# Masked attention over tokens: where the normalised tokens of the next batch are turned, and a new order of the side work

## The chip, the cores and the metric

One core of a Trainium2 chip runs the whole program. The metric is the device time of one execution in microseconds (us); lower is better. The kernel before took 1127.6 us, the median of three runs (1122.86 to 1130.42).

## The reference

Eight batches of 1024 tokens with 256 features pass through one masked attention layer with eight heads of 32, all in float32:

```
h = max(layernorm(x), 0)
q, k, v = h @ Wq + bq, h @ Wk + bk, h @ Wv + bv
scores = q k^T / sqrt(32) + (1 - adj) * -1e9
out = x + softmax(scores) v @ Wo + bo
```

`adj` is one mask of 1024 by 1024 for all batches and heads.

## The kernel before

A batch has two phases, g = 0 and g = 1, of four heads each. A phase has 32 rows: eight query tiles of 128 tokens times four heads. Eight rows are a unit (two query tiles), so a phase has four units. I write a row as its number in the phase, 0 to 31.

For each row TensorE computes 128 x 1024 scores (`scores`, L726), VectorE adds the mask and takes the row's minimum (`mask_row`, L565), ScalarE takes the exponential (L476), TensorE turns the result in eight squares of 128 (`turn`, L759) into two PSUM tiles, and these are copied to SBUF: `turned_a` always by ScalarE (L481), `turned_b` by ScalarE in the rows that `ACT_COPIES` names (L486) and by VectorE in the others (L572). At the first row of the next unit TensorE multiplies the eight turned rows with the values (`heads`, L810). In front of each row's work stand the scores of a row some four places later (`SCORES_AHEAD`), so scores of row 35, which is row 3 of the next phase, are issued in row 31.

The sums of the exponentials are inverted and turned by VectorE at the unit's row `INV_ROW` (L601, L603), go by GpSimd's DMA queue to DRAM (L438) and come back spread over partitions (`inv_t`, four DMAs, L444); VectorE multiplies with them at row `NORM_ROW` of the next unit (`norm_heads`, L609). I call this the inverse chain.

Beside this, each phase holds the projections for the phase that follows, as steps of four pieces that `STEPS` puts at rows: `("qk", s, rows)` computes q (even s) or k (odd s) of the tokens' half s // 2, `("v", s, rows)` the values of a half, `("o", u, rows)` the output of unit u. All go through one PSUM bank, `ps_side`. For a qk step ScalarE writes the high part (L491), VectorE the low part (L577, `lo_done`), and SyncE (SP) then copies the parts to `q_stack` or `k_stack` by 16 DMAs, four for each head h (`stack_step`, L296). The scores of a phase's first four rows wait for their head's part of both halves; the k part of the second half is step qk 3, the last to come. For an o step VectorE adds the residual (`finish`, L615), and SP stores the result, waits until it is stored, and loads the next residual (`store`, L315 to L323).

SP works through its queue in the order of `STEPS`. The next batch's tokens `xn` come by one DMA of 1 MB after the stack of step qk 1 of phase 1 (`load_x`, L305). VectorE takes their moments (L591, L593) in phase 0 at the rows in `STATS`; GpSimd normalises them after unit 2 of phase 0 (`norm`, L412); TensorE turns them in 16 squares of 128 (`turn_ht`, L782) at rows 29 and 30 of phase 0 and 4 and 6 of phase 1 (`HT_ROWS`); ScalarE copies them with a maximum with 0 into `ht` (L508), four copies a batch. The steps qk and v of phase 1 read `ht` for the next batch.

## Time and profile before

| | us |
|---|---|
| median of three runs | 1127.6 |
| lowest, highest | 1122.86, 1130.42 |
| the profiled execution | 1129.57 |
| its span | 1127.8 |
| rows start (end of the start stage) | 33.5 |

The profiled execution's span is the time from its first to its last instruction. The granted TensorE clock was 0.992 of full over it. A batch in the middle of the program takes about 135.5 us, a phase some 67 to 68. In the timeline each line is start, time taken, engine, line, operation, tiles and count; PEld is TensorE's weight load, and since each matmul follows its load, the first weight load of a `turn` marks the start of a row on TensorE.

### The profile page before, as it was taken

How to read it: one execution, taken by the hardware profiler on the slowest of the kernel's cores; microseconds unless marked ns; L12 is line 12 of the kernel's file. 1: busy time of each engine (PE TensorE's matmuls, PEld its weight loads, DVE VectorE, ACT ScalarE, POOL GpSimd, SP SyncE). 2: the span in 40 equal slices, each digit the busy share in tenths (PEclk: the TensorE clock that was granted, in tenths of full speed). 3: DMA queues.
4: the chain of work that ended last, by engine and by line, in shares of the span. 5: the costliest groups of instructions: out<-in, count | busy, mean ns of one | idle time of the engine just before them, and what ended most of it. 6: DMA issues, size and time to landing. Idle time of an engine off the chain costs nothing.

```text
span 1127.8 us, 28288 instructions
## 1 busy us (share of the span) xinstructions
PE 1103.4 (98%) x10672; PEld 890.5 (79%) x10672; DVE 958.4 (85%) x1796; ACT 998.9 (89%) x1835; POOL 314.4 (28%) x508
## 2 busy tenths in 40 slices
PE   7989999999999999999999999999999999999997
PEld 5777887888778878887887887888877888878775
DVE  4788988988989888998889987898988988988884
ACT  2789999999989988999999998999989999999985
POOL 6364212232214212242212412124122142112222
PEclk9999999999999999999999999999999999999999
DMA  6842352425424253332524325243352424424101
GB/s 201 247 110 49 94 139 63 106 62 139 103 71 106 65 134 87 90 97 70 137 67 117 81 76 131 68 111 78 86 140 69 107 67 100 106 61 111 49 27 49
DMA packets 88037, 109.07 MB, mean 97 GB/s; under 512 B 24416, under 2 KB 50144, under 8 KB 87904
## 3 DMA queue, kind: packets, MB, share of 16 engines
q1 hardware_dynamic: 76704, 95.89, 31.6%
q0 software_dynamic: 11008, 11.13, 5.1%
q8 instruction: 86, 1.41, 0.6%
q14 instruction: 47, 0.39, 0.1%
q10 hardware_dynamic: 192, 0.26, 0.1%
HBM read 30.54 MB, written 9.44 MB: 35 GB/s over the span
## 4 chain that ended last, share of the span: by engine, by line
PE 37%; issue 29%; DMA 19%; POOL 10%; DVE 1%; ACT 1%; SPq 0%; POOLq 0%; DVEq 0%; ACTq 0%
PE ps_turn L759 11%; DMA inv_t<-inv_rows 9%; DMA inv_rows<-inv_turned 9%; PE ps_scores L726 9%; PE ps_heads L810 8%; POOL inv_t L444 6%; PE ps_side L766 3%; PE ps_side L793 2%; POOL xn L412 2%; PE ps_side L775 2%; POOL mask L451 2%; POOL ln_t L397 1%; DVE rows L565 1%; DMA mask<-in_adj 1%; ACT rows L476 1%
## 5 line engine op out<-in xcount | busy, mean ns | idle before, releaser
L565 DVE CUSTOM_DVE_ANT_0 rows<-ps_scores,mask 128x1024 f32<-128x1024 f32 x512 | 615.6, 1217 | 36.1 <-PE ps_scores L726 30.5
L476 ACT ACTIVATE rows<-rows,row_min 128x1024 f32<-128x1024 f32 x512 | 589.7, 1159 | 10.9 <-DVE row_min L565 10.8
L759 PE MATMUL ps_turn<-ident_r,rows_raw 128*128 128x128 f32 x4096 | 468.3, 258 | 13.3 <-DVE turned_b L572 7.9
L759 PEld LDWEIGHTS ps_turn<-ident_r,rows_raw 128*128 128x128 f32 x4096 | 402.0, 141 | 89.9 <-ACT rows L476 26.1
L481 ACT ACTIVATE turned_a<-ps_turn 128x512 f32<-128x512 f32 x512 | 307.6, 601 | 90.9 <-PE ps_turn L759 90.7
L726 PE MATMUL ps_scores<-k_stack,q_stack 128*128 128x512 f32 x1016 | 330.6, 424 | 0.5 <-DVE row_min L565 0.2
L572 DVE COPY turned_b<-ps_turn 128x512 f32<-128x512 f32 x312 | 214.9, 689 | 87.1 <-PE ps_turn L759 82.0
L438 POOL DMA_DIRECT2D inv_rows<-inv_turned x64 | 46.4, 725 | 635.5 <-DVE inv_turned L603 630.1
L444 POOL DMA_DIRECT2D inv_t<-inv_rows x256 | 135.5, 536 | 144.0 <-DMA inv_rows<-inv_turned 139.7
L726 PEld LDWEIGHTS ps_scores<-k_stack,q_stack 128*128 128x128 f32 x1016 | 159.3, 188 | 18.2 <-DVE row_min L565 8.8
L810 PE MATMUL ps_heads<-turned_a,v 128*32 128x256 f32 x2048 | 123.8, 382 | 0.4 <-ACT turned_a L481 0.4
L810 PE MATMUL ps_heads<-turned_b,v 128*32 128x256 f32 x2048 | 122.2, 379 | 0.0
L486 ACT ACTIVATE turned_b<-ps_turn 128x512 f32<-128x512 f32 x200 | 120.0, 600 | 0.4 <-PE ps_turn L759 0.4
L476 ACT ACTIVATION_READ_ACCUMULATOR rows<-rows,row_min 128x1 f32 x512 | 105.8, 207 | 0.0
L810 PEld LDWEIGHTS ps_heads<-turned_b,v 128*32 128x32 f32 x2048 | 66.6, 110 | 43.9
L810 PEld LDWEIGHTS ps_heads<-turned_a,v 128*32 128x32 f32 x2048 | 60.0, 109 | 38.0 <-ACT turned_a L481 0.5
L793 PE MATMUL ps_side<-wo,heads_t 128*128 128x256 f32 x256 | 72.6, 389 | 0.7 <-DVE heads_t L609 0.7
L775 PEld LDWEIGHTS ps_side<-wv,ht 128*128 128x128 f32 x496 | 67.6, 191 | 7.1 <-issue 0.4
L775 PE MATMUL ps_side<-wv,ht 128*128 128x128 f32 x496 | 69.4, 276 | 0.0
L766 PE MATMUL ps_side<-ht,wk 128*128 128x256 f32 x240 | 65.2, 395 | 0.0
L766 PE MATMUL ps_side<-ht,wq 128*128 128x256 f32 x240 | 64.9, 389 | 0.0
L793 PEld LDWEIGHTS ps_side<-wo,heads_t 128*128 128x128 f32 x256 | 47.6, 192 | 9.5 <-issue 1.2
(84 smaller groups left out, 592.0 us busy)
## 6 DMA issues: line engine op xcount, KB each, us to landing
q_stack<-q_hi SPq DMA_DIRECT2D x248, 64.0 KB, 2.0
q_stack<-q_lo SPq DMA_DIRECT2D x248, 64.0 KB, 2.1
k_stack<-k_hi SPq DMA_DIRECT2D x242, 64.0 KB, 2.0
k_stack<-k_lo SPq DMA_DIRECT2D x242, 64.0 KB, 2.0
res<-in_x SPq DMA_DIRECT2D x32, 256.0 KB, 2.8
inv_t<-inv_rows POOLq DMA_DIRECT2D x256, 32.0 KB, 2.3
out<-res SPq DMA_DIRECT2D x32, 256.0 KB, 2.4
xn<-in_x SPq DMA_DIRECT2D x7, 1024.0 KB, 6.9
```

What stands on the lines that cost most here:

```text
L444: pool.dma_start(inv_t[h * HEAD_DIM:(h + 1) * HEAD_DIM, :, :], by_head[h].partition_broadcast(HEAD_DIM)).then_inc(inv_in, 16)
L476: nc.scalar.activation(rows[:, k, :], rows[:, k, :], ACT.Exp, bias=row_min[:, k:k + 1], scale=-1.0, accum_out=row_sum[:, u % 2, j:j + 1]). ...
L481: nc.scalar.activation(turned[0][:, place(i // UNIT_ROWS, i % UNIT_ROWS)], ps_turn[0][:], ACT.Copy).then_inc(copied_a, 1)
L486: nc.scalar.activation(turned[1][:, place(i // UNIT_ROWS, i % UNIT_ROWS)], ps_turn[1][:], ACT.Copy).then_inc(copied_b, 1)
L565: nc.vector.tensor_tensor_reduce(out=rows[:, k, :], in0=ps_scores[n % 2][:], in1=mask[:, qt, :], scale=1.0, scalar=START_MIN, op0=ALU.add, ...
L572: nc.vector.tensor_copy(turned[1][:, place(i // UNIT_ROWS, i % UNIT_ROWS)], ps_turn[1][:]).then_inc(copied_b, 1)
L726: mm = nc.tensor.matmul(ps_scores[n % 2][:, c * BANK:(c + 1) * BANK], q_stack[g][:, h, qt * P:(qt + 1) * P], k_stack[g][:, h, c * BANK:(c ...
L759: tr = nc.tensor.transpose(ps_turn[half][:, k, :].bitcast(F32R), rows_raw[:, n % RING, kt * P:(kt + 1) * P], ident_r[:])
L766: mm = nc.tensor.matmul(bank[:, cols], w[n][:, k, g * P:(g + 1) * P], ht[:, k, s // 2 * BANK:(s // 2 + 1) * BANK][:, cols], start=(k == 0) ...
L775: mm = nc.tensor.matmul(bank[:, t * P:(t + 1) * P], ht[:, k, tok], w["v"][:, k, g * P:(g + 1) * P], start=(k == 0), stop=(k == DCH - 1))
L793: mm = nc.tensor.matmul(ps_side[:, t * DIM:(t + 1) * DIM], lhs, w["o"][:, g, :], start=(g == 0), stop=(g == PHASES - 1))
L810: mm = nc.tensor.matmul(ps_heads[h * HEAD_DIM:(h + 1) * HEAD_DIM, 0:UNIT_Q] .rearrange("p (t n) -> p t n", n=P), v[g][:, half * PARTS + kt ...
```

## The change

Batch 0's tokens are still turned by TensorE. For batches 1 to 7:

- `xn` is loaded in four DMAs of 256 KB with eight neighbouring tokens in each partition (`x_p`), one behind each head's part of the stack of step qk 2 of phase 1.
- Moments are taken at rows 0, 0, 1, 7, 7, 8, 8, 9. GpSimd normalises in two halves after units 0 and 1: it subtracts the mean with a maximum with 0, and multiplies in a second instruction, 16 a batch instead of 8.
- VectorE turns squares of 32 in four instructions of 128 x 512 (`turn_squares`), at the ends of rows 23, 24, 24 and 25 of phase 0. A ring of three buffers holds them; the fourth waits until the first is out.
- SP writes them to DRAM (`tokens_t`), two DMAs of 128 KB for each of the four, one pair behind each head's part of the stack of step qk 3 of phase 0, and reads the first half of `ht` back behind the last one, after all writes have landed. The second half is read at the start of phase 1. TensorE waits for these reads in place of `ht_done`.
- The 16 turns on TensorE and four copies on ScalarE a batch are gone.

For all batches: `inv_t` comes by two DMAs of 128 partitions, not four of 32; `INV_ROW` is 7 and `NORM_ROW` 3 (its place within the row moves from the end to the start); four late mask tiles go from GpSimd to VectorE at rows 9, 11, 13 and 15 of the first phase; `turned_b` is copied by ScalarE in 30 rows a batch instead of 25; the steps of phase 0 and the places in a row are laid newly.

```diff
-MASK_AHEAD = (4, 4, 3, 3, 3, 3, 3, 3)
-EXP_AHEAD = (1, 3, 2, 2, 2, 2, 2, 1)
+MASK_AHEAD = (4, 4, 4, 3, 3, 4, 4, 4)
+EXP_AHEAD = (1, 2, 2, 2, 2, 2, 2, 1)
...
-    (("qk", 0, (2, 2, 3, 3)), ("qk", 1, (5, 5, 6, 6)), ("o", 2, (9, 10, 11, 11)), ("qk", 2, (13, 13, 14, 14)),
-     ("v", 0, (17, 18, 19, 19)), ("qk", 3, (21, 21, 22, 22)), ("v", 1, (25, 26, 27, 27)), ("o", 3, (28, 29, 29, 30))),
+    (("v", 0, (1, 2, 3, 3)), ("qk", 0, (5, 5, 6, 6)), ("qk", 1, (9, 10, 11, 11)), ("qk", 2, (13, 13, 14, 14)),
+     ("o", 2, (17, 18, 19, 19)), ("qk", 3, (21, 21, 22, 22)), ("o", 3, (25, 26, 27, 27)), ("v", 1, (29, 29, 30, 30))),
...
-HT_ROWS = {(0, 29): 0, (0, 30): 1, (1, 4): 2, (1, 6): 3}
-HT_UNITS = {(0, 3): 2, (1, 0): 4}
...
+SQUARE_ROWS = (23, 24, 24, 25)
+PAIR, SQUARE_RING = 2, 3
...
 ACT_COPIES = (
-    (2, 5, 6, 10, 13, 14, 17, 18, 21, 22, 26, 28, 29),
-    (0, 1, 2, 10, 13, 14, 18, 21, 22, 26, 29, 30),
+    (2, 3, 5, 7, 8, 10, 11, 13, 15, 19, 21, 23, 26, 27, 29, 31),
+    (3, 5, 7, 8, 11, 13, 15, 16, 19, 21, 23, 27, 29, 31),
 )
...
+            def squares_out(b, pair):
+                n = (b - 1) * SQUARES + pair
...
+                sp.wait_ge(squares_done, n + 1)
+                for j in range(PAIR):
+                    block = pair * PAIR + j
+                    sp.dma_start(tokens_t[block * SQUARE:(block + 1) * SQUARE, :].rearrange("i (c n) -> c i n", c=PARTS),
+                                 squares[:, n % SQUARE_RING, j, :]).then_inc(ht_out[n % SQUARE_RING], 16)
+
+            def ht_back(b, c):
...
+                for k in range(DCH):
+                    sp.dma_start(ht[:, k, cols], tokens_t[k * P:(k + 1) * P, cols]).then_inc(ht_in[c], 16)
...
                     sp.wait_ge(scores_done, row(b, g, 0) + 1)
+                    if g == 1 and b + 1 < BATCH:
+                        ht_back(b + 1, 1)
                     for kind, s, _ in steps(g, b == 0, b == BATCH - 1):
                         if kind == "qk":
-                            stack(nb, ng, s)
...
+                            sp.wait_ge(lo_done, qk_step(nb, ng, s) + 1)
+                            for h in range(PARTS):
+                                stack_step(sp, ng, s, stacked["qk"[s % 2]][ng], range(h, h + 1))
+                                if g == 1 and s == 2 and b + 2 < BATCH:
+
+                                    sp.wait_ge(squares_done, (b + 1) * SQUARES)
+                                    load_x(b + 2, h)
+                                if g == 0 and s == QK_STEPS - 1 and b + 1 < BATCH:
+                                    squares_out(b + 1, h)
+                            if g == 0 and s == QK_STEPS - 1 and b + 1 < BATCH:
+                                ht_back(b + 1, 0)
...
+            def turn_squares(b, pair):
+                n, at = (b - 1) * SQUARES + pair, pair * PAIR * SQUARE
+                dve.wait_ge(normed, (b + 1) * TILES)
+                if n >= SQUARE_RING:
+
+                    dve.wait_ge(ht_out[n % SQUARE_RING], n // SQUARE_RING * PAIR * 16)
+                nc.vector.transpose(squares[:, n % SQUARE_RING].rearrange("p c (j t) -> p t c j", t=TILES),
+                                    xn[:, :, at:at + PAIR * SQUARE].rearrange("p t (c i) -> p t c i", i=SQUARE)
+                                    ).then_inc(squares_done, 1)
```

How the order moves, at three places. First SP's queue in phase 0 of a middle batch, at the store of unit 2 of the batch before. Before, the store stands between the stacks of k (step qk 1) and q (step qk 2):

```order
L296 DMA k_stack<-k_hi 32x512 x2
L296 DMA k_stack<-k_lo 32x512 x2
L317 DMA out<-res 128x2x256
L308 DMA res<-in_x 128x2x256
L296 DMA q_stack<-q_hi 32x512
L296 DMA q_stack<-q_lo 32x512
```

Now it stands between the stacks of q (step qk 2) and k (step qk 3), and the writes of the squares stand in the k stack:

```order
L311 DMA q_stack<-q_hi 32x512
L311 DMA q_stack<-q_lo 32x512
L329 DMA out<-res 128x2x256
L324 DMA res<-in_x 128x2x256
L311 DMA k_stack<-k_hi 32x512 x2
L311 DMA k_stack<-k_lo 32x512 x2
L346 DMA tokens_t<-squares 4x32x256 x2
L311 DMA k_stack<-k_hi 32x512 x2
L311 DMA k_stack<-k_lo 32x512 x2
L346 DMA tokens_t<-squares 4x32x256 x2
```

The store has moved one stack later, and three pairs of square writes stand ahead of the last head's k parts.

Then TensorE's queue at rows 29 to 31 of phase 0 of a middle batch. Before:

```order
L759 MATMUL ps_turn<-ident_r,rows_raw 128x128 x8
L782 MATMUL ps_heads<-ident_r,xn_raw 128x128 x4
L793 MATMUL ps_side<-wo,heads_t 128x256 x2
L759 MATMUL ps_turn<-ident_r,rows_raw 128x128 x8
L726 MATMUL ps_scores<-k_stack,q_stack 128x512 x2
L782 MATMUL ps_heads<-ident_r,xn_raw 128x128 x4
L793 MATMUL ps_side<-wo,heads_t 128x256
L759 MATMUL ps_turn<-ident_r,rows_raw 128x128 x8
L726 MATMUL ps_scores<-k_stack,q_stack 128x512 x4
```

Now:

```order
L821 MATMUL ps_turn<-ident_r,rows_raw 128x128 x8
L837 MATMUL ps_side<-wv,ht 128x128 x4
L821 MATMUL ps_turn<-ident_r,rows_raw 128x128 x8
L788 MATMUL ps_scores<-k_stack,q_stack 128x512 x2
L837 MATMUL ps_side<-wv,ht 128x128 x4
L821 MATMUL ps_turn<-ident_r,rows_raw 128x128 x8
L788 MATMUL ps_scores<-k_stack,q_stack 128x512 x4
```

Both groups of four token turns are gone, and step v 1 stands where step o 3 stood.

Last VectorE's queue from the low part of step qk 3, in row 23, to row 26 (ISA is `mask_row`). Now:

```order
L619 SCALAR_TENSOR_TENSOR k_lo<-ps_side,bk_col,k_hi 128x512
L646 STREAM_TRANSPOSE squares<-xn 128x8x64
L614 COPY turned_b<-ps_turn1 128x512
L607 ISA rows,row_min<-ps_scores0,mask 128x1024
L607 ISA row_min 128x1
L646 STREAM_TRANSPOSE squares<-xn 128x8x64 x2
L614 COPY turned_b<-ps_turn1 128x512
L607 ISA rows,row_min<-ps_scores1,mask 128x1024
L607 ISA row_min 128x1
L646 STREAM_TRANSPOSE squares<-xn 128x8x64
L607 ISA rows,row_min<-ps_scores0,mask 128x1024
```

The four turns are new there; two of them stand in row 24, where TensorE multiplies with the values.

## Rows read from the trace of the kernel before

**Rows 1.** The page, first section: engine, busy us (share) and instructions.

```profile
PE 1103.4 (98%) x10672; PEld 890.5 (79%) x10672; DVE 958.4 (85%) x1796; ACT 998.9 (89%) x1835; POOL 314.4 (28%) x508
```

**Rows 2.** Timeline of TensorE's weight loads, second batch, phase 0, rows 27 to 31.

```profile
228.15 0.77 PEld L759 LDWEIGHTS ps_turn<-ident_r,rows_raw 128*128 128x128 f32 x8
...
229.77 0.77 PEld L759 LDWEIGHTS ps_turn<-ident_r,rows_raw 128*128 128x128 f32 x8
...
233.80 0.87 PEld L759 LDWEIGHTS ps_turn<-ident_r,rows_raw 128*128 128x128 f32 x8
234.62 0.40 PEld L782 LDWEIGHTS ps_heads<-ident_r,xn_raw 128*128 128x128 f32 x4
...
235.72 0.87 PEld L759 LDWEIGHTS ps_turn<-ident_r,rows_raw 128*128 128x128 f32 x8
...
238.51 0.76 PEld L726 LDWEIGHTS ps_scores<-k_stack,q_stack 128*128 128x128 f32 x4
```

**Rows 3.** Groups by line: busy us, mean ns of one, idle before.

```profile
L572 DVE COPY turned_b<-ps_turn 128x512 f32<-128x512 f32 x312 | 214.9, 689 | 87.1 <-PE ps_turn L759 82.0
...
L412 POOL TENSOR_SCALAR xn<-xn,ln_neg_mean,ln_rstd 128x256 f32<-128x256 f32 x56 | 30.2, 555 | 0.8
...
L508 ACT ACTIVATE ht<-ps_heads 128x512 f32<-128x512 f32 x30 | 18.2, 608 | 0.0
...
L782 PE MATMUL ps_heads<-ident_r,xn_raw 128*128 128x128 f32 x120 | 14.2, 242 | 0.0
...
L603 DVE STREAM_TRANSPOSE inv_turned<-row_inv 128x32 f32<-128x32 f32 x64 | 13.6, 212 | 2.2
```

**Rows 4.** Busy time by stretch: batches 1, 4 and 6, counted from 0.

```profile
171.90:307.60 135.70, 134.99 (x1329) 109.59 (x1328) 119.08 (x224) 124.45 (x230) 35.18 (x59) 1.00 0.38 97
...
578.50:716.20 137.70, 136.35 (x1329) 110.77 (x1328) 119.14 (x224) 124.58 (x230) 35.29 (x60) 0.99 0.37 92
...
851.60:986.00 134.40, 134.40 (x1329) 109.61 (x1328) 119.06 (x224) 124.16 (x230) 35.27 (x60) 1.00 0.35 88
```

**Rows 5.** Waits, whole span: us in total, times, longest.

```profile
DVE heads_t L609 <- DMA inv_t<-inv_rows: 8.9, 6, 2.1
```

**Rows 6.** Waits from 33 to 72 us, in the first phase.

```profile
PE ps_turn L759 <- DVE turned_b L572: 4.3, 3, 2.1
```

**Rows 7.** Timeline of SP's queue, phase 0 of the second batch.

```profile
184.21 0.52 SPq L296 DMA_DIRECT2D q_stack<-q_hi  x1
...
195.31 1.21 SPq L296 DMA_DIRECT2D k_stack<-k_hi  x2
...
205.45 0.58 SPq L317 DMA_DIRECT2D out<-res  x1
210.03 0.37 SPq L308 DMA_DIRECT2D res<-in_x  x1
210.45 0.52 SPq L296 DMA_DIRECT2D q_stack<-q_hi  x1
...
223.16 1.14 SPq L296 DMA_DIRECT2D k_stack<-k_hi  x2
...
232.55 1.23 SPq L296 DMA_DIRECT2D k_stack<-k_lo  x2
```

**Rows 8.** Timeline of VectorE in the same phase: ends of rows 12 and 23.

```profile
200.22 0.68 DVE L615 TENSOR_TENSOR res<-ps_side,res 128x512 f32<-128x512 f32 x1
...
222.38 0.75 DVE L577 SCALAR_TENSOR_TENSOR k_lo<-ps_side,bk_col,k_hi 128x512 fp32r<-128x512 f32 x1 [0.24 <-ACT k_hi L491]
```

**Rows 9.** The page, DMA issues: count, KB each, median us from issue to landing.

```profile
k_stack<-k_hi SPq DMA_DIRECT2D x242, 64.0 KB, 2.0
...
res<-in_x SPq DMA_DIRECT2D x32, 256.0 KB, 2.8
...
out<-res SPq DMA_DIRECT2D x32, 256.0 KB, 2.4
```

**Rows 10.** The page, DMA queue: packets, MB, share of 16 engines' span.

```profile
q1 hardware_dynamic: 76704, 95.89, 31.6%
```

More of the change, by code:

```diff
@@ L49 @@
 HT_STEPS = DCH * CHUNKS
-INV_ROW, NORM_ROW = 6, 2
+INV_ROW, NORM_ROW = 7, 3
 PLACES = 1 + UNIT_ROWS
@@ L358, in _ @@
             load_mask(3, MASKS_LATE, TILES)
-            load_x(1)
+            for piece in range(X_PIECES):
+                load_x(1, piece)
             load_res(0, 0)
@@ L534, in slot @@
                         exp(m)
-                row_before = (g, i - 1) if i else (0, ROWS - 1)
-                if row_before in HT_ROWS and not last and (g or i):
-                    copy_ht(b + 1, HT_ROWS[row_before])
                 if kind == "qk" and HIGH_AT[r] == 1:
@@ L661, in slot @@
                 ended = step_ended(b, g, i)
+                if r == NORM_ROW and not (first and u == 0):
+                    norm_heads(unit(b, g, u) - 1, *((g, u - 1) if u else (1 - g, UNITS - 1)))
                 if r == INV_ROW:
@@ L675, in slot @@
                     take(*ended)
-                if r == NORM_ROW and not (first and u == 0):
-                    norm_heads(unit(b, g, u) - 1, *((g, u - 1) if u else (1 - g, UNITS - 1)))
                 for t in range(TILES):
-                    if g == 0 and i == max(STATS[t], 0 if b else UNIT_ROWS) and not last:
+                    if g == 0 and (STATS if b else STATS_FIRST)[t] == i and not last:
                         moments(b + 1, t)
+                for pair in range(SQUARES):
+                    if g == 0 and SQUARE_ROWS[pair] == i and not last:
+                        turn_squares(b + 1, pair)
+                for t in range(MASKS_LATE, TILES):
+                    if first and MASK_ROWS[t - MASKS_LATE] == i:
+                        dve.wait_ge(mask_in[3], 16)
+                        nc.vector.tensor_scalar(mask[:, t, :], mask[:, t, :], 1.0, -MASKED, ALU.subtract, ALU.mult
+                                                ).then_inc(mask_late_ready, 1)
             def tail():
@@ L862, in slot @@
                         heads(unit(b, g, u) - 1, u + 1, g if u else 1 - g, half)
-                if (g, i) in HT_ROWS and not last:
-                    s = HT_ROWS[g, i]
-                    pe.wait_ge(normed, (b + 1) * TILES + (s // DCH + 1) * PARTS)
-                    pe.wait_ge(heads_normed, unit(b, g, u))
-                    pe.wait_ge(ht_done, (b + 1) * HT_STEPS + s)
-                    for t in range(PIECES):
-                        turn_ht(s, t)
                 kind, s, pieces = side_work(g, i, first, last)
```

112 lines of the change are left out of this document (64 added, 48 removed), and 2 rows, old and new, of the table STEPS.

## The prediction

> **What bounds the kernel now.** I read the busy shares first: TensorE's matmuls are busy 98% of the span, ScalarE 89%, VectorE 85%, GpSimd 28% [rows 1]. That a busy matmul unit is also a full one shows only in the order of its weight loads. In the timeline, row 27 starts 1.62 us after row 26 (229.77 after 228.15), and nothing in it is idle: eight turns, two score matmuls and four value matmuls follow each other at once [rows 2]. So TensorE is the bound in the middle of the program, and what it no longer issues comes off the time, as long as no other queue becomes late. What still delays it stands in the waits and in the stretches by batch. `norm_heads` waited six times, 8.9 us in all, for the DMA that brings the inverses back [rows 5]. The stretch of batch 6, the first in which no `xn` is loaded, is 134.4 us; batch 1 takes 135.7 and batch 4 takes 137.7 [rows 4]. The 1 MB load stands in front of the four `inv_t` DMAs of one unit in each batch that has it.
>
> The third view is SP's queue. One stack of 16 DMAs takes 11.1 us to issue (184.21 to 195.31), the next one 10.1 us, and the last of the phase 10.6 us (223.16 to the end of the issue at 232.55). The store between them holds the queue 4.6 us, from 205.45 to 210.03, until the result is stored [rows 7]. SP is thus a queue that is nearly as long as a phase, and its order decides when a head's k parts land.
>
> **The change, part by part.**
>
> *Turns and copies of the tokens.* Four token turns take about 0.34 us of TensorE: eight turns take 0.77, and the row that holds four token turns is 1.92 us long (233.80 to 235.72) where the like one without them is 1.62, so 0.30 is the lower and the group's own 0.40 the upper end [rows 2]. Of the 120 turns in `ps_heads` 112 go, 28 groups of four [rows 3]: 28 x 0.34 = 9.5 us saved (8.4 to 11.2). ScalarE loses 28 copies of 608 ns [rows 3] and gets 5 more copies of `turned_b` a batch at a like price: even. VectorE loses those five, at 689 ns, and gets four turns of 128 x 512. The trace has no turn of that size: below stands the one of 128 x 32 at 212 ns, above a plain copy of the same 128 x 512 at 689 ns [rows 3]; I take 0.65, as the sizes are the same. That is 2.6 us more against 3.4 us less a batch, even again, and two of the four lie in row 24, where VectorE has no turned square to wait for.
>
> *Norm.* GpSimd gets 8 more instructions of about 555 ns a batch, 31 us in all [rows 3]. It is busy 28% [rows 1], and the work lies behind each inverse chain's issues, with rows 16 to 22 as cover. Nothing; were the cover gone, 4.4 us a batch would delay the first squares.
>
> *The token load.* It comes in quarters, behind each head of the stack of qk 2, which starts some 2 us after the inverse is turned; the `inv_t` DMAs are issued before most of it. I expect the five waits of the middle batches to go. Five of the six waits at a mean of 8.9 / 6 = 1.5 us [rows 5], and the 1.3 us by which batch 1 is longer [rows 4], give five times 1.4: 7 us saved (0 to 9). The chain has one row less of time, but two issues fewer: even.
>
> *First phase.* TensorE waited 4.3 us there for `turned_b`, 2.1 of it once, in row 1, where VectorE did two masks before the copy [rows 6]. The copy now comes first: 2 us saved (0 to 4). The mask tiles on VectorE take part of what else is there.
>
> *SP's queue in phase 0.* Here I expect the loss. Step qk 1 now ends in row 11, so its low part stands where the result of unit 2 stood, and ends at about 200.9 in the clock of the second batch [rows 8]. From there SP has, without a pause: the stack of qk 1 (10.6), the stack of qk 2 (10.6), the store with its wait and the next residual (about 3.9: landing is 2.4 at the median [rows 9], and 4.6 was seen behind a stack [rows 7]). The stack of qk 3 starts at 226.0, though its low part is ready at 223.1 (222.38 + 0.75) [rows 8]. Ahead of the last head's end stand 16 issues (10.6) and six square writes; each issue costs 0.37 to 0.63 us in this queue, I take 0.55, 3.3 in all. The last k part is issued at 239.3 and lands 2.0 later [rows 9], at 241.3. TensorE wants it for the scores of row 35 in row 31, at 238.51 before [rows 2], less two groups of token turns, 0.7: 237.8. It waits 3.5 us, and nothing hides that, since its queue is in order and its rows are full. Batches 1 to 6: 21.0 us. Batch 0 has no stores, so its stack starts at 223.1: 0.6. Batch 7 has the store but no squares: 0.2. Together 21.8 us lost (0, if all three stacks go at 10.1, the store at 2.4 and the writes at 0.4; 45, if each is at its upper end and the squares land slowly).
>
> Two more waits lie inside this one. The fourth turn on VectorE waits for the first squares to be out, near 231.6, and holds masks of rows 30 and 31 back by some 2 us; TensorE would wait about 1.5 us for them, less than for the k parts. The first half of `ht` is read after the last squares have landed (242.9), and lands near 246.3 (two issues and 2.8 [rows 9]); TensorE asks for it in row 1 of the next phase, behind all of row 0. That is on time by about a microsecond, and only because the rows before it are late.
>
> The Trainium skill (DMA: Bandwidth & Descriptors, section Issuing engines are not separate DMA queues) says that the time a sequencer takes to initiate a DMA is usually small relative to the DMA itself. By that the stack would cost next to nothing to issue and the sum would be 1109 us; the rows disagree, with about 0.6 us of issue to 2.0 us of landing, sixteen times in a row.
>
> **Sum.** 1129.6 (the profiled execution) - 9.5 - 7 - 2 + 21.8 = 1132.9. That execution is 2.0 above the median of the runs, so for the median: **1131 us**.
>
> **Rivals.**
>
> *A, the gains come through.* If SP's issues go at their quickest, or the steps end a row earlier than I think, the k parts are on time. For it: the last stack has had some 3 us of slack (last issue at about 233.2, 2.0 to land, asked for at 238.51) [rows 2, 7, 9]; against: the store stood one stack earlier, and six writes come on top. Time: 1131 - 21.8 = 1109.
>
> *B, slower: the square writes use few DMA engines.* Their DRAM side has an outermost count of 4 (4x32x256), where all of SP's transfers before had 32 or 128. If the 128 KB are then shared by four engines instead of 16, each moves 32 KB. The queue's packets took 0.316 x 16 x 1127.8 us / 76704 = 74 ns for 1.25 KB [rows 10], 59 ns a KB: 1.9 us for one write, 3.8 for a pair, and 0.95 for the head's own stack on those engines, 4.7 against the 3.7 us in which SP issues them. After three pairs the last head is 3 us later than above, and that decides as soon as the four engines need more than SP's 3.7. Seven batches: 21 us more, 1152; at the quickest packets only some 7 more, 1138. The trace has no such transfer. The Trainium skill (DMA: Bandwidth & Descriptors, section Why a DMA increments its semaphore by 16 and not by 1) says that a DMA is spread over the largest number of engines up to 16 that divides the outermost size of both sides; that rule would give four here, and no run so far shows it.
>
> *C, VectorE or the inverse chain falls behind.* The new places could make waits of the size now seen, 1.5 us [rows 5], once or twice a batch with the forecast's own: about 1142. Against it, nothing in the loads of the engines has changed by more than 1 us a batch.
>
> **Chances.** Forecast 0.38 (own range 1118 to 1142), A 0.22, B 0.27, C 0.08, others 0.05. A change of 1%, 11 us, is about what a measurement of this kernel can tell from none. Faster by over 1% (below 1116): A's 0.22 less its upper edge, and the lower edge of the forecast: 0.25. Slower by over 1% (above 1139): most of B, the upper edge of the forecast, half of C: 0.35. Within: 0.40. The range reaches from A's 1107 to B's 1153.
>
> **What would show it.** Right: in the middle batches TensorE's scores of row 35 (or 34) wait for the DMA of `k_stack` in row 31 of phase 0 by 2 to 5 us, phase 0 is by 2 us and more longer than phase 1; SP's queue has no pause from row 12 to the reads of `ht`. For A: no such wait, and batches of about 133 us. For B: the writes land 4 us and more after issue, where the stores take 2.4, and the reads of `ht` hold row 1. The load: `norm_heads` no longer waits in unit 2 of phase 1, and batch 6 is no shorter than the others. The transposes: 0.65 us each; if they take over 1 us, VectorE is late in row 25. Wrong altogether would be the forecast if TensorE waited in rows 1 to 22 of a middle batch by more than 1 us in sum.

## The result, and the profile after

| | before | changed |
|---|---|---|
| median | 1125.23 us (4 runs) | 1167.63 us (4 runs) |
| lowest, highest | 1122.79, 1130.42 | 1163.76, 1174.87 |
| profiled execution's span | 1127.8 | 1161.6 |
| granted TensorE clock over it | 0.992 | 0.979 |

The ratio of changed to before is 1.037, with a 95% interval of 1.0336 to 1.0405: slower by some 42 us. Ratios are of the fast executions alone: one of four with the 4x32x256 writes below (1615.61 us, clock 0.556) and one of ten without the token turns (3123.74 us) are left out. The predicted 1131 us and its range up to 1153 both missed; the sign of the loss and its place (phase 0 of the middle batches) were in the text, its size was not.

The page of the changed kernel, first section, which answers to [rows 1]:

```profile
PE 1108.7 (95%) x10560; PEld 892.0 (77%) x10560; DVE 957.5 (82%) x1788; ACT 1010.4 (87%) x1847; POOL 345.6 (30%) x481
```

No engine has more to do than before in a way that matters. TensorE issues 112 matmuls less and is busy 95% instead of 98%, so the loss is waiting. The windows of the two phases of a middle batch (the third) show in which half (columns: length; busy time and count of PE, PEld, DVE, ACT, POOL; clock; DMA share; GB/s):

```profile
316.20:389.60 73.40, 69.31 (x658) 56.12 (x657) 63.10 (x121) 63.56 (x117) 31.92 (x45) 0.95 0.36 92
389.60:456.70 67.10, 66.79 (x658) 54.14 (x657) 56.11 (x103) 62.09 (x115) 10.66 (x14) 1.00 0.49 125
```

Before, this batch took 135.6 us (67.4 and 68.2). Over batches 1 to 6, phase 0 has become 4.5 to 6.5 us longer, and phase 1 is 1.3 us shorter in the mean (from 3.8 shorter in batch 4 to 0.9 longer in batch 6). The first phase went from 71.4 to 79.7 us, the last from 75.1 to 77.7. The rows start at 30.5 us instead of 33.5, so the first phase ends 5.3 us later.

What ended the waits, over the whole span of the changed kernel (us in total, times, longest):

```profile
PE ps_scores L788 <- DVE row_min L607: 25.4, 16, 3.9
DVE squares L646 <- DMA tokens_t<-squares: 24.8, 7, 4.7
...
DVE heads_t L664 <- DMA inv_t<-inv_rows: 10.5, 6, 7.2
...
DVE stats L636 <- DMA xn<-in_x: 9.3, 3, 4.8
```

VectorE waits once in each of the seven batches for the ring of squares, 24.8 us in all, and TensorE waits 25.4 us for the masks that stand behind. The timeline of VectorE in the third batch shows one of the seven:

```profile
367.76 1.14 DVE L646 STREAM_TRANSPOSE squares<-xn 128x512 f32<-128x512 f32 x1
...
370.49 2.18 DVE L646 STREAM_TRANSPOSE squares<-xn 128x512 f32<-128x512 f32 x2
...
378.35 1.09 DVE L646 STREAM_TRANSPOSE squares<-xn 128x512 f32<-128x512 f32 x1 [4.03 <-DMA tokens_t<-squares]
379.30 1.20 DVE L607 CUSTOM_DVE_ANT_0 rows<-ps_scores,mask 128x1024 f32<-128x1024 f32 x1
```

and SP's queue beside it, which answers to [rows 7]:

```profile
366.23 0.58 SPq L329 DMA_DIRECT2D out<-res  x1
370.01 0.37 SPq L324 DMA_DIRECT2D res<-in_x  x1
370.43 1.15 SPq L311 DMA_DIRECT2D k_stack<-k_hi  x2
371.62 1.22 SPq L311 DMA_DIRECT2D k_stack<-k_lo  x2
372.95 1.19 SPq L346 DMA_DIRECT2D tokens_t<-squares  x2
...
382.98 1.22 SPq L311 DMA_DIRECT2D k_stack<-k_lo  x2
384.24 1.23 SPq L346 DMA_DIRECT2D tokens_t<-squares  x2
390.31 0.83 SPq L358 DMA_DIRECT2D ht<-tokens_t  x2
```

The first squares are ready near 368.9, but SP is held by the store until 370.0, issues one head's k parts, and starts their writes at 372.95. VectorE's wait for them ends at 378.35, 4.7 us after the second one's issue began. The reads of `ht` wait from 385.5 to 390.3 for the last pair. The fourth turn, the mask behind it and TensorE (which resumes at 380.66 after 3.24 us) follow. Then comes what no term of the prediction held. TensorE's windows before, at and after the moment it resumes:

```profile
376.40:379.60 3.20, 1.02 (x10) 0.79 (x8) 1.25 (x2) 0.77 (x2) 0.00 (x0) 1.00 0.56 147
379.60:386.40 6.80, 5.45 (x24) 4.49 (x25) 5.96 (x11) 3.47 (x6) 0.00 (x0) 0.50 0.57 145
386.40:389.60 3.20, 3.20 (x28) 2.98 (x28) 2.22 (x6) 2.67 (x5) 0.17 (x1) 1.00 0.24 75
```

From 379.6 on, while TensorE still stands, the granted clock is 0.50 (1.2 GHz instead of 2.4) for 6.8 us, in which TensorE is busy 5.45: some 2.7 us of work done twice as slowly. There are seven such windows between row 24 of the first phase and the last phase, 34.1 us in all, with TensorE busy for 29.9 of them. By an estimate (half of that busy time) they cost 15 us of this execution; before, one window of 3.4 us cost 1.7.

### The profile page after: what moved, and what is told of

Read it like the earlier page. It is cut to its first block, busy times and chain, and to the rows that moved or that the text cites. A ratio compares the mean times of both kernels' runs of the same rounds, so it can differ in the third digit from the quotient of the medians.

```text
span 1161.6 us, 28191 instructions
## 1 busy us (share of the span) xinstructions
PE 1108.7 (95%) x10560; PEld 892.0 (77%) x10560; DVE 957.5 (82%) x1788; ACT 1010.4 (87%) x1847; POOL 345.6 (30%) x481
## 4 chain that ended last, share of the span: by engine, by line
PE 34%; issue 23%; DMA 20%; SPq 13%; POOL 7%; DVE 3%; ACT 0%; POOLq 0%; DVEq 0%; ACTq 0%
SPq L311 12%; PE ps_turn L821 11%; PE ps_scores L788 8%; DMA inv_rows<-inv_turned 8%; DMA inv_t<-inv_rows 7%; PE ps_heads L869 6%; PE ps_side L828 4%; PE ps_side L837 2%; POOL inv_t L493 2%; POOL xn L457 2%; PE ps_side L855 2%; DMA tokens_t<-squares 2%; POOL xn L462 1%; DMA xn<-in_x 1%; DVE rows L607 1%
## 5 line engine op out<-in xcount | busy, mean ns | idle before, releaser
L821 PE MATMUL ps_turn<-ident_r,rows_raw 128*128 128x128 f32 x4096 | 472.6, 259 | 13.3 <-DVE turned_b L614 8.1
L821 PEld LDWEIGHTS ps_turn<-ident_r,rows_raw 128*128 128x128 f32 x4096 | 406.7, 142 | 94.7 <-issue 31.0
L788 PE MATMUL ps_scores<-k_stack,q_stack 128*128 128x512 f32 x1016 | 333.5, 428 | 26.2 <-DVE row_min L607 25.4
L614 DVE COPY turned_b<-ps_turn 128x512 f32<-128x512 f32 x272 | 186.9, 687 | 122.0 <-PE ps_turn L821 121.7
L788 PEld LDWEIGHTS ps_scores<-k_stack,q_stack 128*128 128x128 f32 x1016 | 161.5, 190 | 44.3 <-issue 29.9
L529 ACT ACTIVATE turned_b<-ps_turn 128x512 f32<-128x512 f32 x240 | 144.6, 603 | 6.9 <-PE ps_turn L821 6.9
L493 POOL DMA_DIRECT2D inv_t<-inv_rows x128 | 86.5, 680 | 168.0 <-DMA inv_rows<-inv_turned 149.2
L869 PEld LDWEIGHTS ps_heads<-turned_b,v 128*32 128x32 f32 x2048 | 66.5, 110 | 44.0
L837 PEld LDWEIGHTS ps_side<-wv,ht 128*128 128x128 f32 x496 | 71.3, 206 | 5.6 <-issue 0.4
L837 PE MATMUL ps_side<-wv,ht 128*128 128x128 f32 x496 | 74.8, 293 | 0.0
L457 POOL TENSOR_SCALAR xn<-xn,ln_neg_mean 128x256 f32<-128x256 f32 x56 | 63.6, 1148 | 0.0
```

The costliest lines, as they stand in the source:

```text
L493: pool.dma_start(inv_t[:, t, :], inv_rows[t * PARTS:(t + 1) * PARTS, :].unsqueeze(1).to_broadcast([PARTS, HEAD_DIM, P])).then_inc(inv_in, 16)
L529: nc.scalar.activation(turned[1][:, place(i // UNIT_ROWS, i % UNIT_ROWS)], ps_turn[1][:], ACT.Copy).then_inc(copied_b, 1)
L614: nc.vector.tensor_copy(turned[1][:, place(i // UNIT_ROWS, i % UNIT_ROWS)], ps_turn[1][:]).then_inc(copied_b, 1)
L788: mm = nc.tensor.matmul(ps_scores[n % 2][:, c * BANK:(c + 1) * BANK], q_stack[g][:, h, qt * P:(qt + 1) * P], k_stack[g][:, h, c * BANK:(c ...
L821: tr = nc.tensor.transpose(ps_turn[half][:, k, :].bitcast(F32R), rows_raw[:, n % RING, kt * P:(kt + 1) * P], ident_r[:])
L837: mm = nc.tensor.matmul(bank[:, t * P:(t + 1) * P], ht[:, k, tok], w["v"][:, k, g * P:(g + 1) * P], start=(k == 0), stop=(k == DCH - 1))
```

## Experiments

All ratios are to runs of the kernel before that were taken together with the run; 0.1% is 1.1 us. First, what the whole path is worth. In this and the next two the later batches' attention uses batch 0's tokens.

**The square path left out.** Turns, writes, reads and TensorE's wait for them:

```diff
-                        ht_back(b + 1, 1)
...
-                                    squares_out(b + 1, h)
...
-                                ht_back(b + 1, 0)
...
-                        turn_squares(b + 1, pair)
...
-                        pe.wait_ge(ht_in[c], (b + 1) * DCH * 16)
```

> The changed kernel with the square turns on VectorE, their writes and the reads of ht left out (the later batches' tokens are those of batch 0; moments and both norm halves stay); all else, the new places and the token load too, is kept. Theory (the squares' path makes nearly all of the loss): the phases 0 of batches 1 to 6 fall from 72 to 74 us to about 66.5, 40 us in all, and the first phase loses the 5 us that it waits in rows 26 to 29: about 1122 us, a little under the kernel before. Rival (the order of SP's queue, as the prediction had it, or the new places themselves cost): TensorE still waits 2 us or more in rows 28 to 31 of each phase 0, and the time stays over 1135 us. What stays in the first phase (about 75 us instead of 71.4) and at the end (77.7 instead of 75.1) is not the squares'.

Measured: 1122.81 us, ratio 0.9951 (0.9929 to 0.9973). Without the path the kernel is 0.5% below before, so the whole loss belongs to the path. The rival (new places) falls as a large cause.

**Turns kept, writes and reads left out,** and with them the wait for the ring:

```diff
...
-                if n >= SQUARE_RING:
-                    dve.wait_ge(ht_out[n % SQUARE_RING], n // SQUARE_RING * PAIR * 16)
```

> The changed kernel with the four square turns kept on VectorE in rows 23, 24, 24 and 25, without the wait for the ring, and with the writes and the reads of ht left out (tokens of batch 0 as in the run before). Theory (the landing of the writes is the larger part): the turns at 1.09 us each put VectorE behind by about 1.5 us in rows 26 to 28, so each phase 0 is about 68 us, and the time is about 1132 us, 10 above the run without turns and 35 below the changed kernel. Rival (VectorE's time for the turns makes the stall): a stall of 3 us and more in row 28 stays, phase 0 is 71 us or more, and the time is 1150 us or more.

Measured: 1126.29 us, 0.9982 (0.9965 to 0.9998), so the turns cost 3.5 us in all seven batches, less than either theory gave, and little more than the noise (the two intervals overlap). Its third batch:

```profile
306.20:373.80 67.60, 66.86 (x657) 54.21 (x656) 62.90 (x121) 63.15 (x117) 31.74 (x44) 1.00 0.35 88
373.80:440.30 66.50, 66.50 (x658) 54.28 (x657) 56.23 (x103) 62.09 (x115) 10.81 (x14) 1.00 0.42 106
```

VectorE has as much to do in phase 0 as in the changed kernel (62.9 against 63.1 us), yet the phase is 67.6 us long, not 73.4. The turns as instructions:

```profile
L637 DVE STREAM_TRANSPOSE squares<-xn 128x512 f32<-128x512 f32 x28 | 31.4, 1168 | 0.0
```

**Writes added back, piece by piece.** These three keep the turns without the ring wait, and SP writes from a buffer that never changes, at the same places: the writes alone, the same with 128 rows outermost on both sides, and writes with reads of `ht` (which bring that buffer's content, so the tokens are not the batch's).

```diff
-                                 squares[:, n % SQUARE_RING, j, :]).then_inc(ht_out[n % SQUARE_RING], 16)
+                                 bo_row[:]).then_inc(ht_out[n % SQUARE_RING], 16)
```

and, for the second one, in addition:

```diff
-tokens_t[block * SQUARE:(block + 1) * SQUARE, :].rearrange("i (c n) -> c i n", c=PARTS)
+tokens_t[block * SQUARE:(block + 1) * SQUARE, :].rearrange("i (c n) -> (i c) n", c=PARTS)
```

> The run with turns only, plus the eight writes of 128 KB a batch at their places in SP's queue, in their shape of 4x32x256, but from a buffer that nobody changes (bo_row), so that VectorE has no ring to wait for; no reads of ht (tokens of batch 0). Theory 1 (the prediction's own step: issue time ahead of the last k parts): TensorE waits 3 to 4 us for k_stack in row 31, seven batches, 1126 + 21 to 25 = 1147 to 1151 us. Theory 2 (the writes on four DMA engines hold the k parts up as well): waits of 5 to 6 us, 1160 us and more. Theory 3 (k parts have slack enough, the ring wait makes the loss): under 1135 us.

> The same with both sides of each write 128 rows outermost. Theory 1 (issue time alone): the same time as f_writes within 5 us. Theory 2 (four engines): 10 us or more below f_writes. Theory 3: the same as f_writes, under 1135 us.

> f_writes with the reads of ht as in the changed kernel (they bring the content of bo_row, not tokens); only the ring wait is missing from the changed kernel. If the ring wait adds nothing beyond what stands behind it (as the run with the late fourth turn suggests): 1165 to 1172 us, with TensorE waiting in row 31 for k_stack and in row 1 for ht. If the ring wait is a loss of its own: 1155 us or less.

| kernel | ratio (95% interval) | step over the row above |
|---|---|---|
| turns only | 0.9982 (0.9965 to 0.9998) | |
| + writes over 128 rows | 1.0144 (1.0101 to 1.0186) | 1.6%, 18 us |
| + writes as 4x32x256 instead | 1.0249 (1.0214 to 1.0284) | 1.05%, 12 us |
| + reads of `ht` | 1.0365 (1.0339 to 1.039) | 1.2%, 13 us |
| + ring wait (the changed kernel) | 1.037 (1.0336 to 1.0405) | 0.05%, inside the intervals |

Writes of either shape have the same instructions and the same bytes in the same queue, so the 18 us are what they cost at their quickest in this order of steps, and the 12 us are their shape. A further run of the 4x32x256 writes has the profile:

> The kernel of f_writes once more, for its profile. If the four engines hold the k parts up: TensorE waits for k_stack in rows 28 to 31 of phase 0 by 1 to 2 us a batch more than in f_writes16, and the k parts land later after their issue than 2.0 us. If not: equal waits for k_stack, and the difference in other rows.

It took 1161.37 us, a little more than the three above (1153.92 to 1160.47). TensorE's waits for k parts that the trace names, with 128 rows outermost, with 4, and with the reads as well:

```profile
PE ps_scores L785 <- DMA k_stack<-k_lo: 3.0, 3, 1.8
```

```profile
PE ps_scores L785 <- DMA k_stack<-k_lo: 9.2, 6, 2.8
```

```profile
PE ps_side L825 <- DMA ht<-tokens_t: 8.0, 7, 1.9
PE ps_scores L785 <- DMA k_stack<-k_lo: 7.6, 6, 1.8
```

These rows give a lower bound, since a score matmul waits for several DMAs at once and part of the time appears as "issue" in front of the same matmuls. The lengths of the rows give the whole: against the run with turns only, rows 28 to 31 of phase 0 (median of batches 1 to 6, from one weight load to the next) are 2.7 us longer with 128 rows outermost and 4.7 us with 4, and with the reads row 1 of the next phase is 1.5 us longer. The expectation that single k parts land later than 2.0 us hardly came true: their median over the whole run is 2.1. But for heads 1 to 3 (of 0 to 3), behind the writes, the landing records of batches 0 to 6 show it. The last of a head's four k parts lands 2.0 to 2.1 us after its issue in the run with 128 rows outermost and 2.6 to 3.1 us with 4, and the whole stack is in after 15.6 and 17.1 us (medians). So the shape of the writes holds the k parts up, as the second theory said.

**The ring wait taken away in the changed kernel itself**, by a later fourth turn:

```diff
-SQUARE_ROWS = (23, 24, 24, 25)
+SQUARE_ROWS = (23, 24, 24, 28)
```

> The changed kernel, with the fourth turn of squares at the end of row 28 instead of 25, nothing else. Theory ring: in row 25 VectorE stands still for 4 us in each middle batch, until the first buffer of the ring is out, the masks behind it come late, and TensorE loses 4 to 5 us in row 28 and then runs at half clock for a while. Then the wait disappears and the time falls. How far is what the two mechanisms disagree on: if only the ring held the rows, by 6 us in each of seven batches, to about 1125; if SP's late k stack stands right behind it (its last head landed at 386.8 in batch 2, where TensorE would ask at about 382.4), by only 2 us a batch, to about 1150, with the wait now in row 31 on the DMA of k_stack.

Measured: 1172.88 us, 1.0375 (1.0327 to 1.0423): nothing gained. In its waits the ring is gone, and the waits that stood behind it are there instead:

```profile
PE ps_side L828 <- DMA ht<-tokens_t: 10.1, 7, 2.9
PE ps_scores L788 <- DMA k_stack<-k_lo: 5.8, 4, 2.2
...
DVE squares L646 <- DMA tokens_t<-squares: 0.7, 1, 0.7
```

**The write's shape changed in the changed kernel** (by the last diff above; squares then lie in another order, so the tokens are mixed; the bytes and the DMAs are as many):

> The changed kernel, with the square writes laid out in DRAM as they stand in SBUF, so that both sides have 128 as outermost size (the tokens come back in another order, so batches 1 to 7 compute with mixed tokens; sizes and counts are the same). Theory four engines: the first pair's landing came 4.7 to 5 us after its issue in eight steps of its semaphore for two DMAs, where a store takes 2.4 to 3.3; with 16 engines it lands in about 2.5 us, VectorE's wait in row 25 falls from 4 to about 1.5 us, and the time by 2.5 to 4 us in each of seven batches, to 1140 to 1150. If the writes are slow for another cause (DRAM, the queue behind them): the same landing and no more than 3 us less in all.

Measured: 1147.34 us, 1.0183 (1.0129 to 1.0238), 20 us less. That is more than the 12 us of the writes alone: this kernel has the reads and the ring wait as well, and they now cost together only 0.4% over the writes alone (1.0144, inside the intervals), where with 4x32x256 they cost 1.2%. Row 1 of the next phase takes 1.48 us in it, as with turns only, so the reads are in time. The page of the changed kernel has no landing time for its writes, that of this one has 2.0 us:

```profile
tokens_t<-squares SPq DMA_DIRECT2D x56, 128.0 KB
```

```profile
tokens_t<-squares SPq DMA_DIRECT2D x56, 128.0 KB, 2.0
```

In the semaphore records of the two traces, each pair of writes makes 10 increments in the changed kernel (in the third batch's first pair two come 1.0 and 1.6 us after the first issue began, the other eight from 3.5 us on), and the pair has landed 4.9 us after the second issue began in the median; with 128 rows outermost there are 32 increments, and 1.84 us (the page's 2.0 counts each from its own issue). The rule of the Trainium skill (DMA: Bandwidth & Descriptors, section Why a DMA increments its semaphore by 16 and not by 1), which the prediction named, gives four engines for a 4x32x256 write, each with an increment when its data has landed, and the trace agrees with it: two early increments and two times four late ones.

**The steps of phase 0 as before.**

```diff
-    (("v", 0, (1, 2, 3, 3)), ("qk", 0, (5, 5, 6, 6)), ("qk", 1, (9, 10, 11, 11)), ("qk", 2, (13, 13, 14, 14)),
-     ("o", 2, (17, 18, 19, 19)), ("qk", 3, (21, 21, 22, 22)), ("o", 3, (25, 26, 27, 27)), ("v", 1, (29, 29, 30, 30))),
+    (("qk", 0, (2, 2, 3, 3)), ("qk", 1, (5, 5, 6, 6)), ("o", 2, (9, 10, 11, 11)), ("qk", 2, (13, 13, 14, 14)),
+     ("v", 0, (17, 18, 19, 19)), ("qk", 3, (21, 21, 22, 22)), ("v", 1, (25, 26, 27, 27)), ("o", 3, (28, 29, 29, 30))),
```

> The changed kernel with the steps of phase 0 in the rows of the kernel before (the store of unit 2 again one stack earlier, q and k of the first half in rows 2 to 6). Theory SP: the last k stack started 2.5 to 3 us after its low part was ready, since the store stood in front of it; now it starts at once, the first squares are out 2.5 us earlier, and TensorE's loss in row 28 falls from about 5 us to 2 or 3: about 20 us less, 1147. If SP's order does not matter and the ring's wait is set by the landing of the writes alone: the same wait of 4 us on VectorE and 1163 to 1168.

Measured: 1164.89 us, 1.0319 (1.0285 to 1.0353). About 0.5% lies in the store's move and the steps laid beside it, at the edge of the noise (1.037 has 1.0336 to 1.0405), and near the second theory's time; the ring wait fell from 24.8 to 13.4 us all the same.

**All three together** (128 rows outermost with mixed tokens, fourth turn in row 28, steps as before):

> The changed kernel with wide writes (mixed tokens), the fourth turn in row 28 and the old steps of phase 0, the writes still in SP's queue between the heads of the k stack. Each of the three alone left a loss of 2.5 to 7 us a batch in rows 28 to 31 or row 1. If they only hid one another: k's last head is issued 3.4 us later than without writes and lands about at 14.5 after its low part, when TensorE asks; loss under 1 us a batch, and about 1125 (the first phase's 8 us remain). If the issue of eight writes in SP's queue is itself too much: 2 us and more a batch in row 31, 1135.

Measured: 1138.13 us, 1.0107 (1.009 to 1.0124), though 1125 was expected where the three only hid one another. Phase 0 is 68.3 to 68.8 us in it, so per batch it is level with before; what is left stands in the first and the last phase (79.3 and 77.9 us). Rows 28 to 31 are 0.4 us longer in the mean of batches 1 to 6 than with turns only, where the run with the writes over 128 rows in the new order of steps had 3.1 us. So the issue of eight writes is not itself too much for SP's queue: it costs what it does because the store and the stack of qk 2 now stand in front of the last stack, as the prediction had it.

**A complete version with the writes on GpSimd's queue.** The DRAM buffer is laid as the squares lie, `ht` is read back by eight DMAs a half, the steps are as before, and the first moments come later:

```diff
-STATS_FIRST = (8, 8, 9, 10, 12, 14, 16, 16)
+STATS_FIRST = (11, 11, 12, 12, 13, 14, 16, 16)
...
+            def squares_out(b, pair):
...
+                pool.wait_ge(squares_done, n + 1)
...
+                    pool.dma_start(tokens_t[block * P:(block + 1) * P, :],
+                                   squares[:, n % SQUARE_RING, j, :]).then_inc(ht_out[n % SQUARE_RING], 16)
```

> The changed kernel with the three suspected costs taken away and nothing left out: the square writes go by GpSimd's queue after the inverse chain of unit 2, laid in DRAM so that both sides have 128 outermost; SP reads them back in 8 DMAs for each half; the steps of phase 0 as in the kernel before; the first phase's moments from row 11. If SP's order, the four engines and the ring are the whole loss of the middle batches: no wait of VectorE for the ring, none of TensorE in rows 28 to 31, both phases of a middle batch at 66.5 us, 133 a batch, and 1108 to 1115 us, faster than the kernel before by over 1%. If moving the tokens through DRAM costs by its traffic alone (other transfers slower): phases of 68 and more and 1125 or above.

Measured: 1150.95 us, 1.0225 (1.019 to 1.0259); the expectation fell. The writes wait behind the inverse's trip, and pairs land 3.1 us after the second issue began in the median. SP's queue is free, but the ring wait came back (7.0 us in five waits), and the first phase is 82.4 us. The phases 0 of batches 1 to 6 are 68.9 to 71.2 us, not 66.5. The later moments alone, in the changed kernel:

> The changed kernel with the first phase's moments at rows 11, 11, 12, 12, 13, 14, 16, 16 instead of 8, 8, 9, 10, 12, 14, 16, 16. In the changed kernel's first phase VectorE stood 4.8 us in row 8 for the load of batch 1's tokens, with the copy of turned_b of row 9 behind it, and TensorE lost 5.6 us in rows 10 and 11. If that is the cause: the first phase is 5 us shorter, the rest unchanged, 1162. If the late masks on VectorE hold it instead: the loss moves to rows 12 to 16 and stays over 4 us.

Measured: 1175.98 us, 1.0449 (1.0426 to 1.0472), 0.8% worse than the changed kernel. The 4 us that VectorE waited for `xn` in row 8 of the first phase are gone, and TensorE stalls 6.5 us in row 12 instead. GpSimd's late mask tiles, moved back to it, did no better:

> The changed kernel with the four late mask tiles of the first phase made by GpSimd after units 0 and 1, as before, instead of by VectorE in rows 9 to 15. Theory (the masks on VectorE are a part of the first phase's 8 us): the first phase falls from 79.7 to 75 us and the time by 3 to 5 us, to about 1163 us. Rival (the first phase is held by the token load in row 8 and by the squares): the same time within 2 us, or slower, since GpSimd is then late with the first norm half.

Measured: 1176.02 us, 1.0415 (1.0367 to 1.0464). Here the timeline of GpSimd has the cause:

```profile
79.09 7.36 POOL L507 TENSOR_SCALAR mask<-mask 128x1024 f32<-128x1024 f32 x2
```

and that of VectorE its effect:

```profile
97.46 1.09 DVE L651 STREAM_TRANSPOSE squares<-xn 128x512 f32<-128x512 f32 x1 [6.97 <-POOL xn L462]
```

Two mask tiles hold GpSimd for over 7 us, after each of two units, and the first turn of squares waits for the tokens. The rival's cause is what the trace shows; in time the run cannot be told from the changed kernel (the intervals overlap).

**Parts of the change in the kernel before.** The token turns and copies left out (batch 0's tokens again):

```diff
-                    copy_ht(b + 1, HT_ROWS[row_before])
...
-                    for t in range(PIECES):
-                        turn_ht(s, t)
```

> The kernel before, without the 16 token turns of TensorE and the four copies of ScalarE in batches 1 to 7 (their projections read the tokens of batch 0, so 112 matmuls and 28 copies are left out). It prices that term of the sum alone. If TensorE's queue is the bound, as I said: 9.5 us less than before, about 1116 us against 1125 (8.4 to 11.2 less). If the copies on ScalarE also held rows back (rows 1 and 4 to 7 of phase 0 had small waits): up to 13 us less. If another engine had bound those rows: under 4 us less.

Measured: 1121.99 us, 0.9948 (0.9926 to 0.997): 6 us, and 3 to 8 by the interval, not 9.5. No profile of it is read. The token load in quarters behind the heads of the stack of qk 2:

```diff
-                            stack(nb, ng, s)
-                            if g == 1 and s == 1 and b + 2 < BATCH:
...
-                                load_x(b + 2)
...
+                            for h in range(PARTS):
+                                stack_step(sp, ng, s, stacked["qk"[s % 2]][ng], range(h, h + 1))
+                                if g == 1 and s == 2 and b + 2 < BATCH:
...
+                                    load_x(b + 2, h)
```

> The kernel before with the load of the next tokens in four DMAs of 256 KB, one behind each head of the stack of step qk 2 in phase 1, instead of 1 MB behind step qk 1. It prices the load's term: if the 1 MB in front of the inverse chain of unit 1 cost the wait of norm_heads in row 18 and TensorE's loss in row 20, both go in batches 1 to 5 and 7 us with them, 1118 against 1125. If the wait had another cause or the quarters meet another transfer: within 2 us of before.

Measured: 1122.15 us, 0.9967 (0.9953 to 0.9981): 4 us, not 7. Its third batch is 67.4 and 67.1 us, and so is every other from batch 1 to 6:

```profile
307.50:374.90 67.40, 67.40 (x666) 54.84 (x665) 61.42 (x121) 62.49 (x116) 21.30 (x37) 1.00 0.32 80
374.90:442.00 67.10, 67.10 (x666) 54.78 (x665) 57.73 (x105) 61.78 (x115) 13.96 (x22) 1.00 0.42 111
```

Of the complete versions this has the lowest ratio, 0.3% below before. And the new inverse chain, with `inv_t` in two DMAs:

```diff
-INV_ROW, NORM_ROW = 6, 2
+INV_ROW, NORM_ROW = 7, 3
```

> The kernel before with only the new inverse chain: INV_ROW 7, NORM_ROW 3, inv_t in two DMAs of 128 partitions instead of four of 32. Theory (it costs at the end of the program alone): the last unit's inverse leaves a row later and TensorE waits some 3 us more for heads_t, with its clock at half for the eight last matmuls; the last phase is 77 to 78 us instead of 75.1, all other phases within 0.5 us: about 1129 us, 3 above the kernel before. Rival (the later chain is also behind in the middle of the program): norm_heads waits in several units, and the time is 1135 us or more. A third possibility: the two DMAs are quicker behind the token load, the five waits of 1.5 us go, and the sum is even.

Measured: 1126.35 us, 0.9979 (0.996 to 0.9999). The end of the program didn't get later (last phase 74.6 us): the expected 3 us fell, and the third possibility comes nearest. `norm_heads` waits 3.7 us in all instead of the 8.9 of [rows 5]. The run changes two things at once, the row in which it asks and the number of DMAs, and does not tell which did it. The phases 1 of batches 1 to 5, 67.9 to 70.3 us before, are 67.4 us here and 67.1 with the quarters: both take away the same wait, so their gains don't add.

## Why the prediction was wrong

*What bounds the kernel.* Right: in the windows of the load in quarters TensorE is busy for the whole of both phases, and the run without the square path is below before.

*Turns off TensorE, -9.5.* Measured with the copies: -6 (0.9948), and the interval reaches -8.3. The 0.34 us a group holds in the rows: row 4 of phase 1 takes 2.11 us with its group before and 1.79 without it in the run with turns only. In the sum the term is a third too large, and no profile shows where the rest went.

*Turns on VectorE, "even".* They take 1.09 us each in a row, not the 0.65 assumed between 212 and 689 ns [rows 3]. The bracket's upper end was too low: a copy of the same size was no bound for a transpose, and this one also writes with a stride of eight elements, which no run varied. It costs 3.5 us in all, a miss in the row but a small one in the sum. The prediction's own remark, that over 1 us would make VectorE late in row 25, holds only in part: row 26 is 0.7 us longer than without turns, and no other row of batches 1 to 6.

*Norm, nothing.* GpSimd takes 1148 and 923 ns for its two instructions, not 555 each. It stayed hidden in the middle batches. In the first phase its cover is thin, as the masks' run showed.

*Token load, -7.* Measured -4. The mechanism was right. In the profiled executions the phases 1 of batches 1 to 5 are 7.1 us shorter, but 3.2 of that is batch 4, where the execution before had 3.4 us at a clock of 0.50; the other four gained 0.8 to 1.2 us each, where the prediction took 1.4.

*First phase, -2.* Wrong by sign: 8.3 us longer, and it ends 5.3 us later. The gain in the first rows came in part (rows 0 to 2 take 6.8 us instead of 8.2). With turns only the phase ends 0.9 us later than before, with writes over 128 rows 1.1 us, with 4x32x256 writes 5.0 us: here too most of the loss is the shape of the writes, since batch 1's squares are written in it. The wait of VectorE for `xn` in row 8, in front of a copy that TensorE needs, is new, but it stands in the runs without writes as well (4.65 and 4.92 us), where the earlier start of the rows nearly makes up for it:

```profile
54.13 0.43 DVE L636 BATCH_NORM_STATS2 stats<-xn 128x6 f32<-128x256 f32 x1 [4.81 <-DMA xn<-in_x]
```

*SP's queue, +21.8.* The step that carried the forecast is confirmed in size: 18 us (12 to 25, from the intervals' ends) for writes at their quickest, and 2.7 us a batch in the rows' medians (3.1 in their mean), against 3.5 predicted. With the old steps it is 0.4, so the store's new place is a part of it, as predicted. Its timing held too: the stack of qk 3 starts at 370.43, 2.6 us after its low part was ready at 367.84 (2.9 predicted), and the issue of its last part starts 13.2 us later (13.3 predicted). What was misplaced is a part of the rows: of the 3.1 us 1.4 stand in row 31, the rest in rows 28 and 30, so earlier heads' k parts are late too.

*The writes' engines.* Rival B's mechanism is what happened, on top, with 12 us where B had 7 to 21. It had been given a chance of 0.27, and so the forecast was the sum without it: the sum lets the writes land in 2.4 us, like a store, and a pair takes 4.9. And B's own price, 1152, held only the late k parts. That the reads of `ht` would hold row 1 stood among its signs, without a price.

*"Two more waits lie inside this one."* This sentence is the step that failed, together with the landing time that it rests on. The two waits were:

- The reads of `ht`, said to be "on time by about a microsecond": they cost 13 us. The last pair lands 4.9 us after issue instead of 2.4, and the reads' own 3.6 us come behind it. With writes over 128 rows they do lie inside (row 1 takes 1.48 us, as with turns only); that run has a ring wait ahead of them, but so has the changed kernel.
- The ring wait, said to be 1.5 us: it is up to 4.7 us and comes first, in row 25. It takes the place of the waits for k parts rather than adding to them: 0.05% more with it, and nothing less without it. What TensorE waits for in the changed kernel's profile as `row_min`, it waits for as `k_stack` and `ht` in the two runs without the ring wait. So the check named in the prediction (scores waiting for k parts in row 31) reads "wrong" in the changed kernel's trace (row 31 takes 1.52 us, as with turns only), and right in the four runs with the new steps, the writes and no ring wait in their way, where row 31 takes 3.1 to 3.5 us.

*The clock.* No term. In phase 0 of the third batch it makes some 2.7 us of the 6, and about 15 us in that execution. These lie inside the prices above: by the same estimate the profile of the writes over 128 rows has 1.7 us of it and that of the 4x32x256 writes 8.5. It is no cause of its own: in batches 1 to 6 a stall of 2.2 to 3.9 us is ahead of each window, and with turns only there is none between row 24 of the first phase and the last phase.

*Together.* From 0.9982 with turns only: 18 + 12 + 13 + 1 = 44 us, and 0.9982 is 2 us below before; 42 are measured. The forecast was 3 us above before, so 39 are missing in it: 12 for the writes' shape, 13 for the reads, 1 for the ring, less 4 that SP's queue was priced too high, and 16.5 because the three gains, 18.5 us in the sum, came out as 2 with the turns paid. That last miss is the largest of them. Why the run without the path is only 5.5 us below before stays partly open. The parts that were run alone (6, 4 and 2 us) would make 12, but the last two overlap. The new places in a row and the first and last phase may take the rest; I have no run that separates these, and the last phase spread from 75.4 to 78.3 us among kernels with the same end.

## What to carry over

Where two waits stand in one engine's path, price both before calling one hidden: removing the one that the profile names moved the time to the other, and only adding the parts one at a time gave each its price, in that order: the reads cost 13 us behind slow writes, and behind quick ones at most a few, the ring wait included. When a rival says that a transfer lands later, price everything that waits for it. Gains that take away the same wait are counted once. Count the outermost rows of both sides of each new DMA, and each DMA's place in its queue. A bracket for a new kind of instruction needs a row of that kind at its upper end, or has to be open there.

## What the runs showed of the hardware

- A pair of 128 KB writes whose DRAM side is 4x32x256 lands 4.9 us after the second issue began (10 semaphore increments), against 1.84 us at 128 rows outermost (32 increments). 64 KB copies issued between such pairs landed 0.5 to 1.1 us later than between the others.
- VectorE turns 128x512 float32 in squares of 32, written with a stride of eight elements, in 1.09 us when two follow each other; a copy from PSUM of that size takes 0.68.
- GpSimd takes 1148 ns for an add with a maximum with 0 on 128x256 float32 and 923 ns for a multiplication alone, where the add with a multiplication took 555 [rows 3].
- In batches 1 to 6 of the changed kernel the granted clock was 0.50 for 3.4 or 6.8 us after each stall of TensorE of 2.2 to 3.9 us. After shorter stalls it was not always: in the run with the write's shape changed, three of 1.4 to 1.6 us in the middle batches had no such window behind them, while in the kernel before one of 1.3 us (at 690 us) had 3.4 us at 0.50 behind it.
